# A two-layer expert kernel: the instruction lists of TensorE, VectorE and ScalarE in another order

## The reference

```
h = gelu(x @ Wi[e] + bi[e])          # 128 -> 512
r = h @ Wo[e] + bo[e] + x            # 512 -> 128
x1 = layernorm(r) * gamma[e] + beta[e]
```

```
h = layernorm(x1) * ln_g + ln_b
h = (h - mean over steps) / sqrt(var over steps + 1e-8)
h = h * softplus(gamma) + beta
probs = softmax(h @ router_w)        # 8 experts, per token
top 2 experts of each token, their gates normed to 1
y = sum over the two: gate * (relu(h @ w1[e] + b1[e]) @ w2[e] + b2[e])
out = x1 + y
```

## Time and profile before

| | |
|---|---|
| median of three runs | 185.32 us (184.08 to 189.36) |
| the profiled execution | 185.13 us |
| its span, first to last instruction | 182.6 us |
| TensorE busy | 155.2 us (85%), 1276 products |
| VectorE busy | 118.0 us (65%) |
| ScalarE busy | 94.5 us (52%) |
| GpSimd busy | 112.1 us (61%) |
| DMA, mean | 202 GB/s, 36.87 MB |
| granted TensorE clock, mean of the span | 0.965 |
| chain that ended last, by engine | PE 44%, DVE 13%, DMA 11%, POOL 10%, issue 7%, ACT 7%, SP's queue 5% |

### The profile page before, as it was taken

The page is one execution under the profiler, slowest core; times in us unless marked ns, Lnnn a source line. Parts: engine busy times, 40 slices in busy tenths (PEclk is TensorE's granted clock), DMA queues, the critical chain, the costliest instruction groups (busy, mean ns, idle before and its releaser), DMA issues.

```text
span 182.6 us, 5126 instructions
## 1 busy us (share of the span) xinstructions
PE 155.2 (85%) x1276; PEld 147.8 (81%) x1276; DVE 118.0 (65%) x560; ACT 94.5 (52%) x311; POOL 112.1 (61%) x172
## 2 busy tenths in 40 slices
PE   6998899999999989598969999999969999993000
PEld 6886799999999978497969998999969999992000
DVE  5626957868999779749958777553434655644073
ACT  3015934495769438556546566656536566560000
POOL 8883013552988998888767753787777754666000
PEclk9999999999999999999999999999999999999655
DMA  2999952999971287456748677956889785171594
GB/s 64 260 276 328 394 184 46 198 281 360 345 207 44 49 248 227 90 161 175 212 102 203 215 203 192 251 140 202 259 244 265 208 249 146 45 255 49 136 396 171
DMA packets 33948, 36.87 MB, mean 202 GB/s; under 512 B 4104, under 2 KB 23376, under 8 KB 33792
## 3 DMA queue, kind: packets, MB, share of 16 engines
q1 hardware_dynamic: 30528, 30.04, 59.2%
q0 software_dynamic: 2912, 6.44, 10.4%
q10 hardware_dynamic: 480, 0.08, 0.2%
HBM read 28.83 MB, written 7.71 MB: 200 GB/s over the span
## 4 chain that ended last, share of the span: by engine, by line
PE 44%; DVE 13%; DMA 11%; POOL 10%; issue 7%; ACT 7%; SPq 5%; ACTq 1%; DVEq 0%; POOLq 0%
PE bank L1518 11%; PE bank L1503 10%; PE bank L1431 5%; POOL pair_rows L607 5%; DMA pair_rows<-rows,slot 4%; PE bank L1413 4%; PE bank L1310 3%; DMA pairs<-pair_rows 3%; POOL root L594 3%; ACT hidden L1156 2%; DMA o_all<-o_rows 2%; PE bank L1324 2%; SPq L403 2%; PE bank L1493 2%; SPq L367 2%
## 5 line engine op out<-in xcount | busy, mean ns | idle before, releaser
L1216 ACT ACTIVATE hidden<-bank,b_c 128x128 f32<-128x128 f32 x156 | 44.3, 370 | 30.0 <-PE bank L1503 29.9
L612 POOL DMA_INDIRECT o_rows<-weighted,dest x39 | 37.6, 963 | 16.5 <-DVE weighted L976 9.2
L1503 PE MATMUL bank<-h_t,win_w 128*128 128x128 f32 x312 | 41.5, 277 | 0.5 <-DVE h_t L954 0.5
L1518 PE MATMUL bank<-w_sb,hidden 128*128 x312 | 41.6, 277 | 0.2 <-issue 0.2
L607 POOL DMA_INDIRECT pair_rows<-rows,slot x32 | 31.8, 993 | 14.4 <-issue 8.2
L1503 PEld LDWEIGHTS bank<-h_t,win_w 128*128 128x128 f32 x312 | 37.9, 192 | 0.9 <-DVE h_t L954 0.8
L1518 PEld LDWEIGHTS bank<-w_sb,hidden 128*128 128x128 f32 x312 | 37.8, 192 | 1.0 <-issue 0.9
L1156 ACT ACTIVATE hidden<-bank,bi_c 128x128 f32<-128x128 f32 x88 | 24.5, 375 | 10.4 <-PE bank L1413 10.4
L973 DVE TENSOR_TENSOR biased<-bank,b_all 128x128 f32<-128x128 f32 x39 | 11.3, 290 | 25.0 <-PE bank L1518 22.9
L1413 PE MATMUL bank<-x_t,win_w 128*128 (+1 forms) x176 | 23.1, 279 | 1.6 <-DVE x_t L744 1.2
L1431 PE MATMUL bank<-wo_sb,hidden 128*128 x176 | 23.2, 275 | 0.0
(11 more groups left out here) (225 smaller groups left out, 212.0 us busy)
## 6 DMA issues: line engine op xcount, KB each, us to landing
win_w<-in_L_cond_exp_w_dram SPq DMA_DIRECT2D x39, 256.0 KB, 3.4
win_w<-in_L_cond_Wi_dram SPq DMA_DIRECT2D x22, 256.0 KB, 8.2
pairs<-pair_rows SPq DMA_DIRECT2D x39, 65.0 KB, 2.7
wo_sb<-in_L_cond_Wo_dram SPq DMA_DIRECT2D x8, 256.0 KB, 6.2
w_sb<-in_L_cond_exp_w_dram SPq DMA_DIRECT2D x8, 256.0 KB, 6.0
o_all<-o_rows SPq DMA_DIRECT2D x4, 512.0 KB, 5.4
y_rows<-y SPq DMA_DIRECT2D x11, 128.0 KB
o_all<-in_x_dram SPq DMA_DIRECT2D x4, 256.0 KB, 5.3
```

The source lines that it names most:

```text
L612: pool.indirect_dma_start(o_rows, bass.IndirectOffsetOnAxis(dest[:, w:w + 1], 0), weighted[:, w % OUTS, :], None).then_inc(o_stored[w % OU ...
L1216: A.activation(hidden[:, w % 3, ft * P:(ft + 1) * P], bank[w % 2][:, ft * P:(ft + 1) * P], ACT.Relu, bias=b1_flat[:, bass.ds(bias, FT)][:, ...
L1503: last = mm(bank[w % 2][:, ft * P:(ft + 1) * P], win_w[:, (NW + w) % RING, ft * P:(ft + 1) * P], h_t[:, w % 3, :], start=True, stop=True)
L1518: last = mm(bank[3 + w % 2][:, 0:D], hidden[:, w % 3, ft * P:(ft + 1) * P], w2_sb[:, bass.ds(expert, FF)][:, ft * D:(ft + 1) * D], start=( ...
```

## The change

The calls in the lists of TensorE, VectorE and ScalarE stand in another order. The same calls are made with the same arguments; no helper, buffer, semaphore or transfer is changed. The loops over windows 14 to 38 are written out, and in TensorE's and VectorE's lists the lead of `turn_pairs`, `up2` and `copy_turned` over `down2` and `weigh` is no longer fixed: there are places with two `up2` or two `down2` in a row. The lists of GpSimd and SyncE are as before. In the diff, the indentation is cut, and the written-out `relu` calls from 12 to 37 are left out:

```
@@ -977,42 +977,43 @@
         .then_inc(s["weighted_ready"], 1)
+film_tables()
 add_out_bias(0, 3)
-film_tables()
-add_out_bias(3, 14)
 late_constants()
-add_out_bias(14, 15)
+add_out_bias(3, 7)
 moments1(0)
-add_out_bias(15, 17)
 shift(0)
-add_out_bias(17, 19)
+add_out_bias(7, 8)
+apply1(0)
+add_out_bias(8, 9)
 moments1(1)
+moments2(0)
+add_out_bias(9, 10)
 shift(1)
-apply1(0)
-add_out_bias(19, 20)
 apply1(1)
-moments2(0)
+add_out_bias(10, 12)
+apply2(0)
 moments2(1)
 moments1(2)
 shift(2)
-apply2(0)
-add_out_bias(20, 21)
 apply1(2)
 apply2(1)
+add_out_bias(12, 15)
 moments2(2)
 moments1(3)
 shift(3)
+add_out_bias(15, 16)
 var_time(0)
 apply1(3)
 apply2(2)
 moments2(3)
+number_rows()
 film(0)
+apply2(3)
 moments1(4)
-shift(4)
-number_rows()
-apply2(3)
 var_time(1)
 choose(0)
+shift(4)
 apply1(4)
 moments2(4)
 place_pairs(0)
...
@@ -1023,89 +1024,136 @@
 choose(1)
 apply1(5)
 moments1(6)
+add_out_bias(16, 17)
 place_pairs(1)
+plan(0)
+shift(6)
+add_out_bias(17, 19)
 moments2(5)
-shift(6)
-plan(0)
 apply1(6)
 var_time(2)
 moments2(6)
 moments1(7)
+apply2(5)
+add_out_bias(19, 20)
 keep_plan(0)
-apply2(5)
 shift(7)
 film(2)
+add_out_bias(20, 21)
 apply1(7)
 moments1(8)
 choose(2)
+moments2(7)
+shift(8)
 apply2(6)
-shift(8)
-moments2(7)
 place_pairs(2)
 apply1(8)
-add_out_bias(21, 22)
+moments1(9)
 moments2(8)
 apply2(7)
-moments1(9)
+add_out_bias(21, 22)
+shift(9)
 apply2(8)
 plan(1)
+moments1(10)
 copy_turned(0)
 var_time(3)
+shift(10)
 copy_turned(1)
+copy_turned(2)
+apply1(9)
 keep_plan(1)
-moments1(10)
-copy_turned(2)
-shift(9)
-shift(10)
-apply1(9)
+moments2(9)
 copy_turned(3)
 film(3)
 weigh(0)
-moments2(9)
+weigh(1)
 choose(3)
+copy_turned(4)
+weigh(2)
 apply2(9)
-copy_turned(4)
-weigh(1)
 place_pairs(3)
 apply1(10)
-weigh(2)
+weigh(3)
 moments2(10)
 copy_turned(5)
-weigh(3)
 copy_turned(6)
+apply2(10)
 weigh(4)
-apply2(10)
 copy_turned(7)
 plan(2)
 copy_turned(8)
 weigh(5)
+var_time(4)
+keep_plan(2)
+copy_turned(9)
 weigh(6)
-copy_turned(9)
-keep_plan(2)
-var_time(4)
 copy_turned(10)
 weigh(7)
+film(4)
+copy_turned(11)
 weigh(8)
-copy_turned(11)
-film(4)
+choose(4)
 weigh(9)
-choose(4)
 copy_turned(12)
-weigh(10)
 place_pairs(4)
 copy_turned(13)
+weigh(10)
+plan(3)
 copy_turned(14)
-plan(3)
+weigh(11)
+keep_plan(3)
 copy_turned(15)
-weigh(11)
+weigh(12)
+weigh(13)
 copy_turned(16)
-weigh(12)
-keep_plan(3)
-weigh(13)
-for w in range(14, NW2):
-    if w + 3 < NW2:
-        copy_turned(w + 3)
-    weigh(w)
+copy_turned(17)
+copy_turned(18)
+weigh(14)
+weigh(15)
+copy_turned(19)
+copy_turned(20)
+weigh(16)
+weigh(17)
+copy_turned(21)
+copy_turned(22)
+weigh(18)
+weigh(19)
+copy_turned(23)
+weigh(20)
+copy_turned(24)
+weigh(21)
+copy_turned(25)
+weigh(22)
+copy_turned(26)
+weigh(23)
+copy_turned(27)
+weigh(24)
+copy_turned(28)
+copy_turned(29)
+weigh(25)
+copy_turned(30)
+weigh(26)
+weigh(27)
+copy_turned(31)
+weigh(28)
+copy_turned(32)
+copy_turned(33)
+weigh(29)
+weigh(30)
+copy_turned(34)
+copy_turned(35)
+copy_turned(36)
+weigh(31)
+weigh(32)
+weigh(33)
+copy_turned(37)
+weigh(34)
+copy_turned(38)
+weigh(35)
+weigh(36)
+weigh(37)
+weigh(38)
 dve.wait_ge(s["y_all_landed"], 16)
 for i in range(4):
...
@@ -1227,23 +1275,23 @@
 gelu(0)
 gelu(1)
 gelu(2)
+copy_subjects()
 gelu(3)
 gelu(4)
 gelu(5)
 gelu(6)
-copy_subjects()
+affine(0)
 gelu(7)
-affine(0)
 affine(1)
+square_time(0)
+affine(2)
+affine(3)
+gelu(8)
 copy_film(0)
-square_time(0)
+affine(4)
 copy_film(1)
-gelu(8)
-affine(2)
+affine(5)
 gelu(9)
-affine(3)
-affine(4)
-affine(5)
 square_time(1)
 gelu(10)
 copy_rows(0)
...
@@ -1252,35 +1300,36 @@
 gelu(12)
 gelu(13)
 copy_rows(1)
+affine(6)
 gates(1)
-affine(6)
 affine(7)
 gelu(14)
 affine(8)
 affine(9)
+gelu(15)
 square_time(2)
-gelu(15)
 gelu(16)
 gelu(17)
+affine(10)
 gelu(18)
+gelu(19)
+affine(11)
 copy_rows(2)
-affine(10)
+gelu(20)
 gates(2)
-affine(11)
-gelu(19)
-gelu(20)
 affine(12)
 affine(13)
+gelu(21)
 affine(14)
 affine(15)
-gelu(21)
 affine(16)
 affine(17)
 square_time(3)
-for w in range(0, 3):
-    relu(w)
+relu(0)
+relu(1)
+relu(2)
+relu(3)
 copy_rows(3)
-relu(3)
 gates(3)
 relu(4)
 affine(18)
...
@@ -1289,14 +1338,41 @@
 relu(6)
 affine(20)
 affine(21)
+square_time(4)
 relu(7)
-square_time(4)
-for w in range(8, 11):
-    relu(w)
+relu(8)
+relu(9)
+relu(10)
+copy_rows(4)
 gates(4)
-copy_rows(4)
-for w in range(11, NW2):
-    relu(w)
+relu(11)
...
+relu(38)
         @block.tensor
...
@@ -1522,10 +1598,10 @@
 up(0)
 up(1)
+down(0)
+sort_subjects()
+down(1)
 up(2)
-sort_subjects()
-down(0)
-down(1)
 up(3)
 down(2)
 down(3)
...
@@ -1535,19 +1611,19 @@
 down(5)
 up(6)
 up(7)
+turn_z(0)
+sort_film()
 down(6)
 down(7)
-turn_z(0)
-sort_film()
 up(8)
 turn_z(1)
+find_numbers()
+turn_z(2)
 up(9)
 down(8)
 down(9)
-turn_z(2)
-find_numbers()
+route(0)
 up(10)
-route(0)
 up(11)
 down(10)
 rank(0)
...
@@ -1557,94 +1633,158 @@
 route(1)
 down(12)
 down(13)
+turn_z(3)
 rank(1)
-turn_z(3)
 up(14)
+up(15)
 turn_z(4)
-up(15)
+down(14)
 up(16)
-down(14)
 down(15)
 turn_plan(0)
+up(17)
 down(16)
-up(17)
 up(18)
+turn_z(5)
 down(17)
-turn_z(5)
+down(18)
+up(19)
 route(2)
-up(19)
-down(18)
+down(19)
+up(20)
 rank(2)
-up(20)
+up(21)
+down(20)
 turn_z(6)
-down(19)
 turn_z(7)
-up(21)
+down(21)
 turn_z(8)
-down(20)
 turn_pairs(0)
-down(21)
+up2(0)
 turn_pairs(1)
+turn_pairs(2)
 turn_plan(1)
-up2(0)
-turn_pairs(2)
 up2(1)
 up2(2)
 turn_pairs(3)
 down2(0)
 down2(1)
+up2(3)
 route(3)
 down2(2)
 turn_pairs(4)
-up2(3)
+down2(3)
 rank(3)
 up2(4)
 turn_z(9)
-down2(3)
+down2(4)
 turn_pairs(5)
-down2(4)
 turn_pairs(6)
 up2(5)
 turn_pairs(7)
 up2(6)
+turn_z(10)
 down2(5)
-turn_z(10)
 turn_pairs(8)
+down2(6)
+turn_plan(2)
 up2(7)
-down2(6)
 turn_pairs(9)
-turn_plan(2)
+up2(8)
 turn_pairs(10)
-up2(8)
+turn_pairs(11)
 down2(7)
+up2(9)
+turn_pairs(12)
 down2(8)
-up2(9)
-turn_pairs(11)
-turn_pairs(12)
 up2(10)
 down2(9)
 route(4)
+up2(11)
 down2(10)
-up2(11)
+turn_pairs(13)
 rank(4)
 up2(12)
-turn_pairs(13)
-turn_pairs(14)
 down2(11)
 up2(13)
+turn_pairs(14)
+down2(12)
 turn_pairs(15)
+turn_plan(3)
 up2(14)
 turn_pairs(16)
-down2(12)
-turn_plan(3)
+turn_pairs(17)
+down2(13)
+down2(14)
 up2(15)
-down2(13)
-for w in range(14, NW2):
-    if w + 3 < NW2:
-        turn_pairs(w + 3)
-    if w + 2 < NW2:
-        up2(w + 2)
-    down2(w)
+turn_pairs(18)
+up2(16)
+down2(15)
+up2(17)
+up2(18)
+turn_pairs(19)
+down2(16)
+turn_pairs(20)
+turn_pairs(21)
+up2(19)
+down2(17)
+up2(20)
+down2(18)
+turn_pairs(22)
+up2(21)
+down2(19)
+turn_pairs(23)
+down2(20)
+turn_pairs(24)
+up2(22)
+up2(23)
+down2(21)
+turn_pairs(25)
+down2(22)
+up2(24)
+down2(23)
+down2(24)
+turn_pairs(26)
+turn_pairs(27)
+up2(25)
+up2(26)
+turn_pairs(28)
+down2(25)
+up2(27)
+up2(28)
+turn_pairs(29)
+down2(26)
+turn_pairs(30)
+up2(29)
+down2(27)
+turn_pairs(31)
+down2(28)
+up2(30)
+turn_pairs(32)
+down2(29)
+turn_pairs(33)
+up2(31)
+up2(32)
+down2(30)
+up2(33)
+turn_pairs(34)
+turn_pairs(35)
+down2(31)
+turn_pairs(36)
+down2(32)
+up2(34)
+turn_pairs(37)
+down2(33)
+up2(35)
+down2(34)
+up2(36)
+turn_pairs(38)
+down2(35)
+down2(36)
+up2(37)
+up2(38)
+down2(37)
+down2(38)
```

26 lines of the change are left out of this document (added).

## The result

The change made the kernel slower: 188.80 us, median of four runs (187.72 to 189.49), against 186.91 us for the kernel before, now over four runs (184.08 to 189.36). The ratio is 1.022, 95% interval 1.011 to 1.032: slower, but whether by over 2% is open. 183.1 us had been predicted, range 180.9 to 186.2.

The account below looks back on a forecast made before the run. TensorE was taken as the bound, its waits set by a chain through GpSimd and SyncE. Savings of 1.3 + 0.2 + 0.36 + 0.2 = 2.06 us from 185.13 gave 183.1 us, range 180.9 to 186.2.

Parts of the forecast that it names:

- Step 1: Start of TensorE's list: down(0) and down(1) ahead of up(2) avoid waiting for a whole GELU; TensorE gains 0.6 us.
- Step 2: First block: turn_z(1) and find_numbers move up; GpSimd's root_time(1) starts at 44.6 us for 45.58.
- Step 3: First scatter of block 1: VectorE's slots come at 54.97 for 55.26, so it starts 0.3 us earlier, at 55.8.
- Step 4: GpSimd from 56 to 84 us stays 0.3 us ahead; TensorE gets ahead and waits 1.65, 1.9 and 0.75 us.
- Rival C: Slower, 187.1 us, chance 0.07: long waits at turn_pairs(5) drop TensorE's clock; route(4) and all behind come 4.0 us later.
- Step 5: Block 2 to its pairs: turn_pairs(5) at 93.45 for 94.11, TensorE waiting 2.4 us instead of 1.46, without loss.
- Step 6: Blocks 3 and 4: scatters at 90.95 and 110.95, the latter 1.3 us earlier; new 1.2 us wait ahead of turn_pairs(11).
- Step 7: SyncE's eleven issues from pairs 21 to pairs 25 take 10.7 us after the scatter; pairs 25 land at 133.75.
- Step 8: From turn_pairs(25) to the last store: fewer small gaps and less store queueing, 0.76 us shorter.
- The rule against it: GpSimd's small roots, sharing SBUF interfaces with VectorE, lose 0.2 us each, 1.4 us over seven; sum 184.5.
- Rivals A and B: A, 0.17: only the end's 0.76 us stay, 184.4; B, 0.20: GpSimd's lead holds and pairs load earlier, 181.3.

Follow-up runs that it names:

- n_new_start: Changed kernel's lists for the first 55 us, the lists of the kernel before behind; 190.80 us, ratio 1.032 to the kernel before.
- n_busy: Changed kernel plus 19 idle TensorE products ahead of turn_z(7), turn_z(8), up2(0) and turn_pairs(2); 188.43 us, ratio 1.012 to the kernel before.
- h_old_start: Lists of the kernel before for the first 55 us, the changed kernel's lists behind; 189.40 us, ratio 1.029 to the kernel before.
- n_copy_first: Changed kernel with VectorE's copy_turned(1) and copy_turned(2) ahead of var_time(3) and shift(10); 188.70 us, ratio 1.017 to the kernel before.
- n_old_steady: Changed kernel with the old even loops over the last 24 windows on TensorE and VectorE; 188.13 us beside 187.25, no ratio.
- c_busy: Changed kernel plus 19 idle TensorE products, in surroundings where the kernel before took 211.16 us; 220.46 us, no ratio.
- e_after_busy: Changed kernel plus 19 throw-away TensorE products, in surroundings where the kernel before took 210.67 us; 220.31 us, ratio 1.051.
- m_both_busy: Changed kernel plus 19 idle products, with route(4), rank(3), rank(4), place_pairs(3) and place_pairs(4) moved ahead; 188.99 us, ratio 1.014 to the kernel before.

## Why the prediction was wrong

*Step 1, start: right.* `up(0)` itself was at 19.05 for 18.55, which is the execution's. Counted from it, `up(3)` comes at 5.41 for 6.08 and `up(8)` at 17.80 for 18.37, so the 0.6 us are there up to `up(8)`; they are in n_new_start and n_busy too. Behind it they are gone: `up(9)` comes at 21.76 for 19.95.

*Step 2, first block: wrong.* Predicted `root_time(1)` at 44.6, measured 45.65; from `up(0)` that is 26.60, for 26.05 predicted and 27.03 before. What stands behind it lost more: GpSimd's `root2(4)`, which the first scatter stands behind, waited 0.76 us for VectorE. I priced `turn_z(1)`, `find_numbers` and `turn_z(2)` by what they wait for and not by what stands behind them on TensorE: `down(8)` and `down(9)` end at 43.93 instead of 41.63 us, and `moments1(4)` with them. The copy of film_b on ScalarE (0.46 us of waiting at `film(0)`) was missed too. From `up(0)` to the first scatter the new order costs 0.74 us, the gain of step 1 taken in; h_old_start gave them back.

*Step 3, the first scatter of block 1: wrong by what came from step 2*: 57.74 for the predicted 55.8.

*Step 4, waits of TensorE: this is the step that failed.* Predicted 1.65, 1.9 and 0.75 us ahead of `turn_z(7)`, `up2(0)` and `turn_pairs(2)`; measured 1.52, 0.39 and 1.88. The sum is 4.3 predicted and 3.8 measured, so the waits were foreseen; their price was put at nothing, since TensorE "gets ahead" there. They brought the clock down to half for 6.8 us. `route(3)`, predicted at 85.05, came at 90.89, and 2.65 us of that are the fall (n_busy). The wait ahead of `turn_pairs(2)` is itself a late input, since `copy_turned(1)` and `copy_turned(2)` stand behind `var_time(3)` and `shift(10)` on VectorE: with them ahead `up2(1)` came 1.7 us sooner by distance (n_copy_first, 31.26 for 32.94). Rival C had the mechanism, but put it behind the 2.4 us wait of step 5, and at 0.07.

*Step 5.* The wait at `turn_pairs(5)` isn't there: TensorE came late itself, at 97.50 for the predicted 93.45.

*Step 6, blocks 3 and 4: wrong, for the most part by what came from step 4.* Predicted scatter of block 3 at 90.95 us, measured 96.63. `choose(3)` was to end at 88.0 and had its last output at 93.90; from there `rank(3)` followed at once. I had let `rank(3)` on TensorE go by, and in this run nothing hangs on that. With the clock up it does: `rank(3)` then stands 0.9 us (n_copy_first) or 1.8 us (n_busy) behind its input, for pairs 4 and `down2(3)`. I had also taken it that a fixed list of SyncE means fixed times, and it doesn't: pairs 4 were issued 3.3 us later in after, 4.2 us later in n_busy. The new wait of 1.2 us ahead of `turn_pairs(11)` is only 0.11 in after, but 1.14 to 1.46 in the five profiles with the new middle and the clock up: right, wherever TensorE is not slow itself. The scatter of block 4, predicted at 110.95, started at 115.70.

*Step 7, SyncE from pairs 21 to pairs 25: right.* 10.77 us, for 10.70, with all the lateness ahead of it handed on:

```profile
124.60 0.33 SPq L412 DMA_DIRECT2D pairs<-pair_rows  x1
...
135.37 0.33 SPq L412 DMA_DIRECT2D pairs<-pair_rows  x1
```

*Step 8, the end: wrong in sign.* Predicted 0.76 us shorter; from `turn_pairs(25)` to the last store it took 33.15 for 32.69 us, and 32.95 to 33.31 in the six other profiles with the new end and the clock up there (32.52 and 32.93 in the two others with the old end). TensorE's last products are a pair of `down2` back to back. The same 270 products take 31.85 for 30.95 us: where two of them start over 0.19 us apart, the excess over the usual 0.11 sums to 1.41 us, for 0.44 in the old list.

*The rule against it* would have made the sum 184.5. GpSimd's small roots took 734 ns in the mean, for 744 before: in these lists nothing of the feared 1.4 us shows. *Rivals A and B* asked whether little or more is won; neither held. The error was of one kind: a wait was priced only where it stood, and not by what the products behind it then cost.

Shown by profiles: the new middle is what loses (n_new_start, h_old_start, one profile each); the fall of the clock makes most of the lateness of block 3 (n_busy, n_copy_first); with the clock up and block 3 moved ahead 1.55 to 2.24 of the 2.77 us come back (three profiles, two of them with block 4 moved too), and with one of the two nothing beyond the spread. Not shown: how much of this is the order and how much the landing ahead of pairs 21; what the idle products cost by themselves; whether an order without them brings the time back. Only argued: the 0.57 us behind the scatter of block 4, and why edits that are small in the profile spread so far in the run times.

## What to carry to other kernels

Idle time of TensorE in a kernel bound by it can have a second price. Where a new order lets TensorE run ahead of its inputs, look for several waits close together, and price the products behind them at half speed too (here 3.79 us for 16 products) before calling the waits free. When an order is changed, follow each input of the engine that carries the chain through every list on which it has a step, here `route(3)` on TensorE, and the load of pairs 4 on SyncE, whose list nobody had touched. And two slow paths of nearly one length can hide each other, so that an experiment on one alone says "no effect": run both edits together before dropping either, and look whether a step that no edit touches has moved as well.

## What the hardware showed that I had not expected

The clock fell after waits of 1.52, 0.43, 0.21, 0.39 and 1.88 us between 74.6 and 83.1 us, with TensorE busy in between, and stayed at half for 6.8 us in the profile of after, for 3.4 us in that of n_old_steady, which has the same lists up to there. After 1.52, 0.43, 0.66 and 0.47 us (n_copy_first) it stayed up; in the kernel before it stayed up through 1.32, 0.94 and 0.45 us. So how long it lasts isn't given by the order alone. The Trainium skill (TensorE: Matmul & The Clock Gate, Part 1) has activity as what releases the clock; the idle products of n_busy agree, the clock held with them. In c_busy and e_after_busy it fell for 3.4 us in spite of them, where a wait of 2.51 and 2.22 us stood.

The granted clock in the rows doesn't tell all of TensorE's speed. In the first 21 us of n_new_start sixteen transposing products took 3.78 us, in m_both_busy 2.05, at a granted clock of 1.00 in both:

```profile
17.28 3.78 PE L1327 MATMUL bank<-perm,o_all 128*128 128x128 f32 x16
```

```profile
12.43 2.05 PE L1400 MATMUL bank<-perm,o_all 128*128 128x128 f32 x16
```

These sixteen are the last of a stretch, and in the two profiles they begin 4.85 us apart already. In all profiles the 128x128 products of a group first start 0.21 us apart, the distance that they have in the dent of after at 0.50. They change to 0.11 us after some 5 us in m_both_busy, at 13.1 in before, between 13.7 and 15.8 in after, and not before 20.6 in n_new_start. In the same order `up(0)` stands at 16.60, 18.55, 19.05 and 21.78 us, and with it goes much of the spread between executions of one kernel. What decides when they change no run shows.
